# Attention reads a transposed copy of x; LayerNorm's mean moves into the weights and its root into the copies of queries and keys

## The reference

```python
xn = layernorm(x, g_in)                                  # (x - mean) * rsqrt(var + EPS) * g_in
q = (xn @ Wq).reshape(b, n, H, DH) * scale
k, v = split(xn @ Wkv)                                   # one head of keys and values, plus a null key and value
sim = einsum('bhid,bjd->bhij', q, k) + bias              # bias: 16 heads x 512 x 512, and the null column
sim = where(causal, neg, sim); sim = where(mask, sim, neg)
out = softmax(sim) @ v -> @ Wo -> layernorm(out, g_out)
xn = out / rms(out) * norm_weight
logits = xn @ router_weight.T + router_bias              # each expert takes its 512 best tokens
y = fc2(gelu(fc1(xn[idx]))); output = weighted mean over the experts that took the token
return x + output
```

## Time and profile before

| | |
|---|---|
| timed runs (3), us | 1983.42, 1986.42 (median), 1990.57 |
| profiled execution: span, us | 1989.2 |
| TensorE busy | 1898.9 us, 95% |
| VectorE, ScalarE, GpSimd busy | 76%, 66%, 61% |
| attention stage, setup included | 0 to 478 us |

### The profile page before, as it was taken

How to read it: one execution, slowest core, us unless ns; L and a number is a source line. 1 busy time by engine, 2 the same in 40 slices (tenths; PEclk the granted TensorE clock), 3 DMA queues, 4 the chain that set the end, 5 groups by cost and what they waited for, 6 DMA issues and landing times.

```text
span 1989.2 us, 41130 instructions
## 1 busy us (share of the span) xinstructions
PE 1898.9 (95%) x12165; PEld 1692.4 (85%) x12165; DVE 1509.7 (76%) x2377; ACT 1317.7 (66%) x2624; POOL 1221.6 (61%) x1229
## 2 busy tenths in 40 slices
PE   4799999998789999999999999999999999999998
PEld 3678888886679899998989899899989889888887
DVE  5678878776888878777787877778787777777764
ACT  4667777753556666766667676767666676766664
POOL 3578888874056747565675846667584756656551
PEclk9899999999999999999999999999999999999999
DMA  6854444435733525254343534344352534434342
GB/s 236 323 152 126 120 130 133 124 82 175 245 97 124 139 101 146 93 150 109 121 118 120 143 98 140 103 136 128 111 151 87 151 92 146 106 132 113 125 120 46
DMA packets 90254, 263.12 MB, mean 132 GB/s; under 512 B 20593, under 2 KB 22353, under 8 KB 85073
## 3 DMA queue, kind: packets, MB, share of 16 engines
q1 hardware_dynamic: 70866, 211.44, 33.0%
q0 software_dynamic: 17024, 34.19, 9.1%
q10 hardware_dynamic: 2304, 16.78, 2.1%
HBM read 223.47 MB, written 55.60 MB: 140 GB/s over the span
## 4 chain that ended last, share of the span: by engine, by line
PE 68%; DVE 4%; ACT 2%; issue 1%; POOL 0%; DMA 0%; DVEq 0%; ACTq 0%; POOLq 0%
PE experts_b_a L2319 18%; PE experts_b_y L252 11%; PE experts_b_y L253 11%; PE experts_b_y L254 11%; PE experts_b_b L2319 9%; PE experts_b_c L2319 4%; ACT experts_h L1815 1%; PE experts_b_turn L2289 1%; DVE experts_x_lo L1969 1%; PE experts_b_c L2308 1%; PE experts_b_turn L2308 1%; DVE experts_h_lo L2042 0%; DVE experts_w_lo L2039 0%; ACT experts_y_out L1749 0%; DVE experts_y_out L2007 0%
## 5 line engine op out<-in xcount | busy, mean ns | idle before, releaser
L252 PE MATMUL experts_b_y<-experts_w_hi,experts_h_hi 128*128 128x512 f32 x1024 | 406.7, 397 | 1.2 <-DVE experts_h_lo L2047 1.2
L1593 POOL TENSOR_TENSOR experts_s_raw<-experts_w_raw 128x256 f32<-128x256 f32 x128 | 146.9, 1147 | 422.8 <-DMA experts_w_raw<-in_w 409.1
L253 PE MATMUL experts_b_y<-experts_w_lo,experts_h_hi 128*128 128x512 f32 x1024 | 403.7, 394 | 0.0
L254 PE MATMUL experts_b_y<-experts_w_hi,experts_h_lo 128*128 128x512 f32 x1024 | 398.9, 390 | 0.0
L2319 PE MATMUL experts_b_a<-experts_x_hi,experts_w_hi 128*128 (+1 forms) x1024 | 289.8, 283 | 5.3 <-ACT experts_p_copy L1774 4.3
L2319 PE MATMUL experts_b_a<-experts_x_hi,experts_w_lo 128*128 (+1 forms) x1024 | 289.7, 283 | 0.0
L2319 PE MATMUL experts_b_a<-experts_x_lo,experts_w_hi 128*128 (+1 forms) x1024 | 289.4, 283 | 0.0
L254 PEld LDWEIGHTS experts_b_y<-experts_w_hi,experts_h_lo 128*128 128x128 f32 x1024 | 192.4, 188 | 43.5
L2319 PEld LDWEIGHTS experts_b_a<-experts_x_hi,experts_w_hi 128*128 128x128 f32 x1024 | 194.2, 190 | 25.6 <-issue 8.3
L252 PEld LDWEIGHTS experts_b_y<-experts_w_hi,experts_h_hi 128*128 128x128 f32 x1024 | 194.3, 190 | 25.3 <-DVE experts_h_lo L2047 1.7
L253 PEld LDWEIGHTS experts_b_y<-experts_w_lo,experts_h_hi 128*128 128x128 f32 x1024 | 194.3, 190 | 20.8
(11 more groups left out here) (383 smaller groups left out, 5547.5 us busy)
## 6 DMA issues: line engine op xcount, KB each, us to landing
experts_w_raw<-in_w SPq DMA_DIRECT2D x256, 512.0 KB, 3.3
bias<-in_bias SPq DMA_DIRECT2D x68, 256.0 KB, 4.2
xn_dram<-wq_hi ACTq DMA_DIRECT2D x16, 1024.0 KB, 10.5
spread_w<-weight_dram SPq DMA_DIRECT2D x32, 512.0 KB, 6.4
attend_q_x<-in_x SPq DMA_DIRECT2D x17, 256.0 KB, 2.9
attend_k_x<-in_x SPq DMA_DIRECT2D x17, 256.0 KB, 6.0
xn_dram<-rows_y_xn SPq DMA_DIRECT2D x17, 256.0 KB, 4.7
experts_b_sb<-in_b SPq DMA_DIRECT2D x16, 256.0 KB, 3.9
```

What stands on the lines that cost most here:

```text
L252: nc.tensor.matmul(out, lh, rh, start=first, stop=False)
L253: nc.tensor.matmul(out, lh, rl, start=False, stop=False)
L254: return nc.tensor.matmul(out, ll, rh, start=False, stop=last)
L1593: nc.gpsimd.tensor_tensor(s1, a21, a22, ALU.add).then_inc(s_done, 1)
```

## The change

A second input `xT` holds x with channels on the partitions, tile by tile. SP loads it as `q_t`, `k_t` beside `q_x`, `k_x`, which serve the statistics alone. ScalarE and VectorE split `q_t`, `k_t` directly; `q_n`, `k_n`, their transposes and the shifts are gone. LayerNorm's mean is taken out of the weights: the setup makes, by products of TensorE in plain float32, the column means of g * W in every partition (`mean_by` holds g / 512), and VectorE subtracts them (`centre`) before the weights are split. The root r is a scale per row of the result, so `keep_queries` and `keep_keys` put it on as they copy: `q_r` and `k_r` are read there, later than before. On GpSimd `key_root` moves behind `out_root`, and `query_root` behind `scale_old(j-4, 0)`. The rest is the order of splits in the first turns, 60 instead of 55 warming transposes, and waits that fit the banks no longer used.

```diff
@@ setup, GpSimd
+                pool.memset(mean_by[:, :, :], 1.0 / D).then_inc(mean_by_done, 1)
+                nc.gpsimd.tensor_tensor(mean_by[:, :, :], mean_by[:, :, :], spread(g_col[:, :], [P, KD, P]), ALU.mult)\
...
@@ setup, TensorE (new), in the block whose end all engines wait for
+                pe.wait_ge(ident_done, 4)
+                for _ in range(40):
+                    nc.tensor.transpose(keep["banks"][1][:, 0:P], keep["ident"][:, :], keep["ident"][:, :])
+                pe.wait_ge(mean_by_done, 2)
+                pe.wait_ge(raw_in[1], 32)
+                for a in (1, 0):
+                    for k in range(KD):
+                        last = nc.tensor.matmul(keep["mean_q"][a], mean_by[:, k, :], keep["wq_raw"][k // 2][:, k % 2, a * 512:(a + 1) * 512],
+                                                start=k == 0, stop=k == KD - 1)
+                    last.then_inc(keep["mean_done"], 1)
...
+                pe.wait_ge(keep["mean_done"], 3)
...
@@ SP
                 def load_query(n):
                     at = number(sp, n, 4, NT - 1)
-                    free(sp, q_normed, n)
+                    free(sp, qx_done, n)
+                    sp.dma_start(q_t[:, :, :].rearrange("p k t -> p (k t)"), io["xT"][bass.ds(at * P, P), :]).then_inc(qt_in, 16)
+                    free(sp, q_half, n)
                     sp.dma_start(q_x[:, :], io["x"][bass.ds(at * P, P), :]).then_inc(q_in, 16)
...
@@ GpSimd
                 def key_root(n):
-                    free(pool, k_normed, n)
+                    free(pool, kv_kept, n)
                     root(n, k_mv[:, 1:2], 1.0, k_r[:, :], k_stats, k_rooted, k_root)
-                    shift(n, k_b[:, :], k_mv[:, 0:1], k_r[:, :], k_root, k_scale)
 
                 def query_root(n):
-                    free(pool, q_normed, n)
+                    free(pool, q_kept[0], n)
+                    free(pool, q_kept[1], n)
                     root(n, q_mv[:, 1:2], 1.0, q_r[:, :], q_stats, q_rooted, q_root)
-                    shift(n, q_b[:, :], q_mv[:, 0:1], q_r[:, :], q_root, q_scale)
...
                     if on(-6):
                         out_root(j - 6)
+                    if on(-1):
+                        key_root(j - 1)
                     if on(-3):
                         carry = number(pool, j - 3, 6, 1)
-                    if on(0):
-                        query_root(j)
                     if on(-3):
                         new_sums(j - 3, carry)
...
                     if on(-4) and not is_last(edge, on, -4):
                         scale_old(j - 4, 0)
+                    if on(0):
+                        query_root(j)
                     if on(-2):
                         mask_bias(j - 2, 3)
...
@@ ScalarE
                 def keep_queries(n, a):
                     free(act, null_ready, n)
                     free(act, q_turned[a], n)
-                    copy(n, flat(q[:, 8 * a:8 * a + 8, :]), b_q[a][:, :], q_ready[a], q_kept[a])
+                    done(act, q_root, n)
+                    done(act, q_ready[a], n)
+                    nc.scalar.activation(flat(q[:, 8 * a:8 * a + 8, :]), b_q[a][:, :], ACT.Copy, scale=q_r[:, :]).then_inc(q_kept[a], 1)
...
@@ VectorE, first turns
+                def centre(raw, k, mean):
+                    nc.vector.scalar_tensor_tensor(raw, raw, keep["g_col"][:, k:k + 1], mean, ALU.mult, ALU.subtract)\
+                        .then_inc(keep["centred"], 1)
...
@@ TensorE
-                    if on(0):
-                        if edge:
-                            pe.wait_ge(qx_done, upto(-1))
-                            pe.wait_ge(q_kept[1], upto(-1))
-                            pe.wait_ge(weight_copied, upto(-3))
-                        pe.wait_ge(biased[3], upto(-2))
-                        query_rows(j)
...
-                    if on(0):
-                        if edge:
-                            pe.wait_ge(kx_done, upto(-1))
-                        pe.wait_ge(y_normed, upto(-5))
-                        key_rows(j)
```

More of the change, by code:

```diff
@@ L688, in keep_keys @@
                     free(act, v_done, n)
-                    copy(n, kkv[:, :], b_kv[:, 0:3 * DH], kv_ready, kv_kept)
+                    done(act, k_root, n)
+                    done(act, kv_ready, n)
+                    nc.scalar.activation(kkv[:, :], b_kv[:, 0:3 * DH], ACT.Copy, scale=k_r[:, :]).then_inc(kv_kept, 1)
                 def key_parts(n):
@@ L759, in fill_pieces @@
                         fill(nc.scalar, keep, piece)
-                for k in range(KD // 2, KD):
-                    split_wq(k)
+                for k in range(KD):
+                    split_wq(1, k)
                 def split_wo(a):
@@ L804, in turn @@
                         query_rows(j)
-                    if on(0):
-                        key_norm(j)
+                        if edge and j == 0:
+                            for k in range(KD):
+                                split_wq(0, k)
+                            split_wkv()
+                            act.wait_ge(keep["hi_done"], 2 * KD + 1)
                         if edge:
@@ L1001, in turn @@
                         begin_max(j - 2)
+                    if edge and on(0) and j == 0:
+                        query_rows(j)
+                        centre_wq(0)
+                        for k in range(KD):
+                            centre(keep["wkv_raw"][:, k, :], k, keep["mean_kv"])
                     if on(0):
                         query_stats(j)
+                        if edge and j == 0:
+                            split_wq(0)
                     if is_last(edge, on, -4):
@@ L1028, in turn @@
                         key_stats(j)
-                        if edge and j == 0:
-                            for k in range(1, KD):
-                                split_first("wq", k)
                     if on(-2):
@@ L1062, in turn @@
                     if on(0):
-                        query_rows(j)
                         if edge and j == 0:
-                            for k in range(KD):
-                                split_first("wkv", k)
+                            split_wkv()
+                        else:
+                            query_rows(j)
                         if edge and j == 1:
@@ L2556, in program @@
                 "lists_done": scope.enter_context(nc.semaphore("lists_done")),
+                "mean_done": scope.enter_context(nc.semaphore("mean_done")),
+                "centred": scope.enter_context(nc.semaphore("centred")),
+                "banks": [scope.enter_context(nc.psum_tensor(f"attend_bank{n}", [P, 512], F32)) for n in range(8)],
                 "const_in": scope.enter_context(nc.semaphore("const_in")),
```

147 lines of the change are left out of this document (74 added, 73 removed).

## The result

The changed kernel takes 2113.38 us (median of 4 runs, 2108.18 to 2125.22) against 1985.92 for the kernel before in the same session: ratio 1.0644, 95% interval 1.0624 to 1.0664. The forecast was 2026, with a range of 2003 to 2062. The direction was right; the growth was 127 us where 40 was forecast. The profiled execution, the slowest of the four, has a span of 2123.5 us and a mean granted clock of 0.955 (before: 1989.2 and 0.988), so the growths read from the two traces come to 134 us.

What follows compares the result with a forecast made beforehand. The prediction took TensorE's list to bound the steady turn before, and the ring after the change. It added 33.9 us for the ring, 3 for loads and 3 for setup, 39.9 on 1986.4: 2026 us, range 2003 to 2062.

Steps and rivals of the forecast that it cites:

- TensorE's list: TensorE's own work in a steady turn, falling from 23.11 to 22.25 us as two groups of four transposes go.
- the ring: Chain of waits from one `keep_queries(·, 0)` to the next, bounding the turn: 2.42 us more in each of 14 turns.
- The two waits: On GpSimd, `query_root` waits for `keep_queries`, idling 4 us, and `key_root` waits for `keep_keys`, costing 0.94 us.
- from there through GpSimd and ScalarE (...): 10.84: Step of the ring from VectorE's new maximum through GpSimd and ScalarE to the end of `keep_keys`: 10.84 us.
- the sum 25.53: Forecast length of the ring, all seven steps added: 25.53 us a turn against 23.11 before.
- rival (a): TensorE's clock also falls each turn, `queries(j, 0)` lasting 2.7 us longer in 12 turns: 2058 us; chance 0.23.
- (b): Rival: part of the ring, above all `key_root`, is hidden; turn 24.6 us, total 2010 us; chance 0.17.
- (c): Rival: TensorE's list stays the bound and the time falls to 1976 us; chance 0.09.
- the step of `key_root`: Step of the ring on GpSimd, handover and root behind `keep_keys`: 0.94 us.
- Moved loads: On SP's queue, `load_query` waits until behind the maximum, and two more 256 KB loads an item join: 3 us.
- the ring's 1.51 step: Step of sums, inverse and second scaling, 1.51 us, said to come later than the weights' moved load.
- The setup: Mean products on TensorE before the barrier end at 21.2 us, up to 3.5 us late; 3 us taken.

Runs made afterwards that it cites:

- experiments 10 and 17: 10: queries on the old path plus own key root, on the changed kernel, 1996.46 us. 17: keys' half alone on the kernel before, own key root, 1992.74 us.
- experiment 16: A separate kernel timing VectorE instructions from PSUM and SBUF, alone and beside GpSimd multiplications; with both operands in SBUF 0.72 us goes to 2.6.
- experiment 6: Changed kernel with 12 and 10 extra identity transposes per loop turn filling TensorE's idle time; 2107.71 us, ratio 1.0597.
- experiment 4: Changed kernel with VectorE's `value_parts` (`v_lo`) moved ahead of `query_parts(.,1)`; 2074.37 us, ratio 1.0413.
- experiment 8: Changed kernel with the load of `q_x` put ahead of the load of `q_t`; 2098.01 us, ratio 1.0563.
- experiment 9: Changed kernel with only the keys new: queries normalised and turned as in the kernel before, no `q_t` load; 2033.30 us, ratio 1.0235.
- experiment 11: Kernel of experiment 9 plus the added load at half its bytes, with its wait for `qx_lo`, read by nothing; 2088.04 us, ratio 1.0496.
- experiment 12: Kernel of experiment 11 with `load_query` moved behind the spread weights on the sync queue; 2114.63 us, ratio 1.0641.
- Experiment 7: Changed kernel with one mean product instead of four in each of three groups in the setup; 2115.95 us, ratio 1.0655.
- experiment 13: Kernel of experiment 1 with `load_query` moved behind the spread weights on the sync queue; 2085.07 us, ratio 1.0488.
- experiment 1: Changed kernel where ScalarE copies the query root for itself and `query_root` waits only for that copy; 2080.92 us, ratio 1.0465.

## Why the forecast had the direction and missed the size

**TensorE's list: right.** 22.25 us a turn plus 0.43 for the queries' transposes gives the 22.7 us that experiments 10 and 17 show. The gain exists, and it is only seen where the ring is open.

**The two waits and the ring: right in mechanism.** GpSimd idles 4.69 us before the root in `q_r`, TensorE before the product on `wq_hi`, `sc` waits for `bias`, as written. Opening the waits gave 33 and 27 us, together 65. Four of seven steps hold within 0.12 us. The other three make up 4.92 of the 5.01 us between 25.53 and 30.54: 2.72, 1.74 and 0.46.

**The step that failed: "from there through GpSimd and ScalarE (...): 10.84", and with it the sum 25.53.** It was read off the old timeline as if the work between the maximum and `keep_keys` would keep its pace. `keep_keys` also waits for `v_lo`, which VectorE reached behind a list that the change itself slowed. It measured 13.56 us. Of the 2.72 us more, 2.65 lie between the maximum and the start of `v_lo` (12.70 against 10.05). Moving `v_lo` alone won 39 us. I had looked at what each wait blocks and not at which instructions of the ring change their operands: `qx_lo` now reads `q_t` in SBUF instead of a PSUM bank. The groups of VectorE's rows between 100 and 440 us, first of the kernel before:

```profile
L956 DVE SCALAR_TENSOR_TENSOR rows_y_xn<-rows_y_xn,attend_y_r,norm_w_row 128x512 f32<-128x512 f32 x13 | 11.9, 912 | 0.0
L834 DVE TENSOR_TENSOR attend_qx_lo<-attend_bank,attend_qx_hi 128x512 fp32r<-128x512 f32 x13 | 8.8, 679 | 0.0
```

and of the changed one:

```profile
L983 DVE SCALAR_TENSOR_TENSOR rows_y_xn<-rows_y_xn,attend_y_r,norm_w_row 128x512 f32<-128x512 f32 x8 | 22.9, 2864 | 0.0
L861 DVE TENSOR_TENSOR attend_qx_lo<-attend_q_t,attend_qx_hi 128x512 fp32r<-128x512 f32 x11 | 16.5, 1501 | 0.0
```

That is 0.82 and 1.95 us more a turn, on means that take in the early turns. `qx_lo` starts at 297.27 while GpSimd's `add_new` runs, ends 0.54 us behind it, and so hands `out_rows` to the long `null_products` (298.09 + 2.83 = 300.92), behind which it ends by 0.54 again. The Trainium skill (SBUF — State Buffer, "SBUF: two separate sides") describes this: VectorE and GpSimd share a port pair as an exclusive lock, for VectorE instructions with two SBUF inputs or in a two-port mode, and whoever comes first holds it for a whole instruction. The rows and experiment 16 agree. The forecast priced these instructions by their old rows.

**The clock, rival (a), came true beside the forecast and not instead of it.** It had 0.23. The clock is at 0.50 twice a turn and `queries(j, 0)` takes 4.44 us, which is 1.57 of the 1.74 us by which its step of the ring is longer. That agrees with the traces of experiment 6 (about 1.5 us a turn) and is less than the 2.7 of the rival, since the first quarter of the group still ran at 1.00. The Trainium skill's case of a kernel that falls back once per tile (TensorE: Matmul & The Clock Gate, "HAM oscillation") fits this trace in kind; its example has one wait a tile, of 3 to 5 us, and here there are two a turn, of 2.10 and 1.70. Idle pieces of 2.09 and 1.31 us in a turn left the clock at 1.00 in experiment 4, pieces of 2.10 and 1.70 did not here. Rivals (b) and (c) are out: nothing of the ring was hidden, and the step of `key_root` took 1.40 instead of 0.94. The chances that the forecast gave also leave 0.13 outside its range, (c) and no change, and not 0.15.

**"Moved loads ... I take 3": far too small.** Undoing one order alone (experiment 8) won 15 us, and the load with its wait cost 55 in a kernel without the query's wait (experiments 9 and 11). The forecast moved the weights' load by a microsecond and said that the ring's 1.51 step comes later still. The load is issued 4.1 us behind the maximum (300.01) instead of 2.0 (202.22). The forecast missed that VectorE's first scaling of the same load stands in front of `v_lo`, and that `query_stats` waits for `q_x`, in front of the masks on GpSimd in the early turns and, in experiment 12, in front of `v_lo` on VectorE.

**The setup: the end of the mean products was forecast at 21.2 and is 20.62,** and a product of 512 columns in plain float32 takes two passes of 0.43 us, the upper bound taken. The next block starts 3.0 us late (21.16, before 18.18). Experiment 7 took back only 1.7 us of it at the first maximum and shows no effect on the total, so whether the 3 us belong in the sum stays open.

What stays open: how much of the 5 us a turn beyond the forecast ring is VectorE's hold-up by itself. In the turn shown VectorE's list alone accounts for the step, since it waits for no load there. But it and the late loads bring `v_lo` at about the same time, so each hides the other: without the hold-up the load was enough to reach 2088, and with it a later load changed nothing that can be measured (experiment 13). The two can't be added. Nor was the rest of the start's growth (7.6 us at the first maximum) taken apart.

## What to carry to other kernels

A ring found in the waits must be summed with the instructions as they will be: for each instruction on it, and each one queued ahead of it on its engine, ask whether the change alters its operands or what runs beside it. A transfer whose buffer is now freed by a later engine moves behind that engine's place in the turn, and everything behind it on its queue moves too; moving it down the queue only picks another consumer to be late. When several late things arrive together, undo them singly and together before naming one: experiment 9, 48 us below experiment 1, seemed to show the port's price, and experiment 11 showed that a load and its wait cost 55 us without it.

## What the runs showed of the hardware

- A VectorE instruction of 512 columns with both operands in SBUF, beside a running GpSimd instruction, ends about 0.54 us behind that instruction (297.27 + 1.40 and 298.60 + 2.86 here, 2.6 us instead of 0.72 in experiment 16). One of 16 columns takes 1.66 instead of 0.17 us there and ends right behind it (31.75; the next GpSimd instruction starts at 31.68). A copy of one SBUF operand is held up too (2.51 instead of 0.43); a subtraction with one operand in PSUM is not (0.72 in both).
- GpSimd is held up in turn: in experiment 16 two of its multiplications of 1024 columns start 2.30 us apart (18.66 and 20.96), and the next 2.75 us later (23.71), once VectorE's SBUF reader had its turn between them.
- The clock fell from 1.00 to 0.50 with two idle pieces of 2.10 and 1.70 us in a turn of 30.5 us, came back after about 3.4 us, and fell again later in the same turn. Each time it fell some 0.8 us after TensorE had gone back to work (302.12 and 312.37; at 1.00 until 302.9 and about 313.1). The 22 transposes of experiment 6 kept it at 1.00 in the turn shown and the six behind it.
